# A selective-scan audio layer with routed experts: in the last group, the router of the group before, its scatters, the weight loads and a partial projection change their places

## The reference, cut to what matters

```python
h = tok(x)                                   # 64 x 128 x 256
h = h + attn(layernorm(h))                   # input projection, causal convolution of 4 taps, SiLU, then
                                             #   state = exp(delta*A)*state + delta*B*x ; y = sum(state*C)
                                             #   over 16 states and 512 channels, + D*x, * silu(z), @ W_out
h = h + ffn(layernorm(h))                    # 8 experts, each row goes to its best two:
# logits = x @ w_gate ; gates = softmax(logits) ; top_k(gates, 2)
# y_e = (silu(x @ wg[e]) * (x @ wi[e])) @ wo[e] ; out += gate_e * y_e
```

## Time and profile before

| | |
|---|---|
| median of 3 runs | 2734.6 us (2734.56 to 2735.72) |
| profiled execution, its own time | 2733.95 us |
| its span | 2732.2 us |
| busy share: TensorE, VectorE, ScalarE, GpSimd | 93%, 73%, 52%, 71% |
| first tile load of the expert stage | 1927.00 us |
| last group's last product ends | 1882.65 us |

### The profile page before, as it was taken

One profiled execution on the slowest core, in us unless ns is written; L12 is line 12 of the kernel. 1 busy time (PEld: TensorE's weight loads), 2 busy tenths in 40 slices (PEclk: granted clock), 3 DMA queues, 4 the chain that ended last, 5 costly groups with the idle time before them and its releaser, 6 DMA issues. The chain is left out here.

```text
span 2732.2 us, 29788 instructions
## 1 busy us (share of the span) xinstructions
PE 2539.4 (93%) x7976; PEld 1282.9 (47%) x7977; DVE 1984.1 (73%) x2171; ACT 1430.7 (52%) x2700; POOL 1945.9 (71%) x960
## 2 busy tenths in 40 slices
PE   4899999999999999999999999976799999999999
PEld 2234444444444444444444444433466666666665
DVE  1699999999999999999999999996222222222222
ACT  1666676766767667676676776752122222222222
POOL 1698999999999999999999999995222222222222
PEclk9999999999999999999999999988899999999999
DMA  1321413314133142241422414315222222222222
GB/s 42 140 113 42 153 60 126 136 34 158 64 117 144 30 157 90 89 148 35 154 110 62 151 39 147 128 39 208 66 46 44 43 45 41 46 45 42 46 44 31
DMA packets 125317, 236.03 MB, mean 86 GB/s; under 512 B 46289, under 2 KB 93426, under 8 KB 108834
## 3 DMA queue, kind: packets, MB, share of 16 engines
q1 hardware_dynamic: 98198, 200.42, 21.3%
q0 software_dynamic: 25984, 34.36, 7.3%
q10 hardware_dynamic: 1036, 0.09, 0.0%
HBM read 182.09 MB, written 53.65 MB: 86 GB/s over the span
## 5 line engine op out<-in xcount | busy, mean ns | idle before, releaser
L555 POOL TENSOR_TENSOR arena<-u,arena 128x2048 f32<-128x2048 f32 x255 | 1155.6, 4532 | 38.6 <-DVE psum L1069 34.5
L1069 DVE TENSOR_TENSOR_SCAN psum<-psum,arena 128x1024 f32<-128x1024 f32 x416 | 950.7, 2285 | 20.4 <-POOL arena L555 12.4
L1509 PE MATMUL psum<-hc,ident 128*128 128x512 f32 x1664 | 810.2, 610 | 106.0 <-DVE hc L1103 106.0
L831 ACT ACTIVATE psum<-delta,a_neg 128x508 f32<-128x508 f32 x1024 | 654.3, 670 | 0.0
L659 POOL DMA_INDIRECT out_dram<-hres,tok_id x135 | 210.1, 1556 | 595.0 <-ACT hres L996 541.1
L1509 PEld LDWEIGHTS psum<-hc,ident 128*128 128x128 f32 x1664 | 299.7, 191 | 508.7 <-issue 267.7
L1103 DVE TENSOR_TENSOR hc<-psum,arena 128x1024 f32<-128x1024 f32 x416 | 507.4, 1220 | 9.1
L1666 PE MATMUL psum<-arena,xnt 128*128 x1080 | 512.4, 597 | 0.0
L1370 DVE COPY z<-psum 128x512 f32<-128x512 f32 x135 | 93.4, 692 | 454.8 <-PE psum L1675 454.8
L825 ACT ACTIVATE psum<-zeros 128x8 f32<-128x8 f32 x512 | 90.3, 176 | 499.3 <-DVE hc L1103 451.2
L996 ACT ACTIVATE hres<-psum,tok_w 128x256 f32<-128x256 f32 x135 | 64.1, 474 | 451.1 <-PE psum L1685 444.4
(11 more groups left out here) (191 smaller groups left out, 2608.1 us busy)
## 6 DMA issues: line engine op xcount, KB each, us to landing
arena<-ssm_rows SPq DMA_DIRECT2D x128, 1024.0 KB, 5.5
delta<-expert_rows SPq DMA_DIRECT2D x135, 129.0 KB, 2.1
h_saved_rows<-hnew SPq DMA_DIRECT2D x16, 512.0 KB, 6.7
hres<-h_saved_rows SPq DMA_DIRECT2D x16, 512.0 KB, 3.5
out_dram<-h SPq DMA_DIRECT2D x16, 512.0 KB, 2.9
draw<-ssm_rows SPq DMA_DIRECT2D x16, 256.0 KB, 3.3
arena<-in_L_ffn_wg_dram SPq DMA_DIRECT2D x8, 512.0 KB, 10.1
arena<-in_L_ffn_wi_dram SPq DMA_DIRECT2D x8, 512.0 KB, 10.5
```

Of the source, the lines that this page charges most:

```text
L555: pool.tensor_tensor(dBx[k % 2], rep, b_rep[:, q * QN:(q + 1) * QN, :], ALU.mult).then_inc(dbx_ready, 1)
L831: last = nc.scalar.activation(o, d, ACT.Exp, scale=a_neg[:, c, n:n + 1])
L1069: nc.vector.tensor_tensor_scan(out_, h, src, 0.0, ALU.mult, ALU.add).then_inc(scan_done, 1)
L1509: last = nc.tensor.matmul(yacc[c % 2], ident[:, :], state[:, i, :], start=False, stop=(nth_sum[k] == LAST_SUM[c] and i == 1))
```

## The change

In the last group alone (`last`), the parts of group 14's router come four half units sooner on ScalarE, VectorE and TensorE (`sooner = 4`), with `norm2`'s second part at half unit 15 and not 16; count and slots, which stood at half unit 31 and in the tail, now stand inside the step at half units 27 to 29. The second partial projection moves from half unit 31, ahead of that unit's sum, to the tail, behind it. GpSimd's `tail` sends all eight scatters of group 14 ahead of the root of the last group. SyncE's first wait for the weight loads now also wants the first four scatters of group 14 to have landed.

```diff
--- before.py
+++ after.py
@@ -441,7 +441,7 @@
 
             def tail(g):
                 load_hres(g, G)
-                free_for(B_AT, (skip_done, NCH * G), (u_ready, NCH * G))
+                free_for(B_AT, (skip_done, NCH * G), (u_ready, NCH * G), (scattered, 16 * (2 * GB * (g - 1) + GB)))
                 free_for(C_AT, (dbx_ready, UN * G))
                 free_for(C_AT + 2 * QN * GT, (hc_ready, NOWN * G - 4), (hc_pool, NPL * G))
                 free_for(X_AT + SCN, (hc_ready, NOWN * G), (scan_done, HU * G))
@@ -639,10 +639,10 @@
                 first_row(g - 1)
                 scatter(g - 1, 0, 0)
                 scatter(g - 1, 0, 2)
-                rsqrt(g, 1, stat2, pow2)
                 second_row(g - 1)
                 scatter(g - 1, 1, 0)
                 scatter(g - 1, 1, 2)
+                rsqrt(g, 1, stat2, pow2)
                 scatter_last(g)
 
             pool.wait_ge(s_const, 9)
@@ -895,6 +895,7 @@
                 softplus_first()
 
             def step(g, par, first, second, more, last):
+                sooner = 4 if last else 0
                 for k in range(HU):
                     if k + 1 < HU:
                         exps(g, k + 1)
@@ -926,13 +927,13 @@
                             softplus_relu(g, 2)
                         if k == 7:
                             softplus_relu(g, 3)
-                        if k in (14, 16):
-                            norm2(g - 1, (k - 14) // 2)
-                        if k in (20, 22):
-                            evac_xn2t(g - 1, (k - 20) // 2)
-                        if k == 25:
+                        if k in ((14, 15) if last else (14, 16)):
+                            norm2(g - 1, int(k > 14))
+                        if k + sooner in (20, 22):
+                            evac_xn2t(g - 1, (k + sooner - 20) // 2)
+                        if k + sooner == 25:
                             router_exp(g - 1)
-                        if k == 30:
+                        if k + sooner == 30:
                             second_gate(g - 1)
                     if not last:
                         if k == 19:
@@ -1236,19 +1238,23 @@
                             residual(g - 1, 0)
                         if k == 10:
                             residual(g - 1, 1)
-                        if k == 24:
+                        if k + sooner == 24:
                             router_max(g - 1)
-                        if k == 26:
+                        if k + sooner == 26:
                             first_keys(g - 1)
-                        if k == 27:
+                        if k + sooner == 27:
                             one_hot(g - 1, 3, 0, dv)
-                        if k == 28:
+                        if k + sooner == 28:
                             second_max(g - 1)
                             exp_inverse(g - 1)
-                        if k == 29:
+                        if k + sooner == 29:
                             second_keys(g - 1)
-                        if k == 30:
+                        if k + sooner == 30:
                             one_hot(g - 1, 11, 1, mask_ready)
+                        if k + sooner == HU:
+                            positions(g - 1)
+                        if k + sooner == HU + 1:
+                            slots(g - 1)
                     if k == 30 and more:
                         aggregate(g + 2, 0, stat1)
                     times_c(g, k)
@@ -1257,17 +1263,22 @@
                             stats2(g - 1)
                         if k == 11:
                             aggregate(g - 1, 1, stat2)
-                        if k == 24:
+                        if k + sooner == 24:
                             router_sub(g - 1)
-                        if k == 26:
+                        if k + sooner == 26:
                             largest_key(g - 1, 2)
-                        if k == 27:
+                        if k + sooner == 27:
                             without_first(g - 1)
                             exp_sum(g - 1)
-                        if k == 28:
+                        if k + sooner == 28:
                             second_equal(g - 1)
-                        if k == 29:
+                        if k + sooner == 29:
                             largest_key(g - 1, 10)
+                        if k + sooner == HU:
+                            new_counts(g - 1)
+                            chosen_positions(g - 1)
+                        if k + sooner == HU + 1:
+                            slots_out(g - 1)
                     if not second:
                         if k == 0:
                             new_counts(g - 2)
@@ -1278,11 +1289,6 @@
                         stats1(g + 2)
 
             def tail(g):
-                positions(g - 1)
-                new_counts(g - 1)
-                chosen_positions(g - 1)
-                slots(g - 1)
-                slots_out(g - 1)
                 gate_y(g, NCH - 1)
                 residual(g, 0, bank_a)
                 residual(g, 1, yacc[0])
@@ -1616,19 +1623,19 @@
                         if k in (29, 30):
                             project_z(g + 1, k - 29, 2 * min(g + 3, G))
                     if not first:
-                        if k in (19, 21):
-                            turn_row(g - 1, (k - 19) // 2)
-                        if k == 23:
+                        if k + sooner in (19, 21):
+                            turn_row(g - 1, (k + sooner - 19) // 2)
+                        if k + sooner == 23:
                             router(g - 1)
-                        if k == 31:
+                        if k + sooner == 31:
                             count(g - 1)
                     if more:
                         if k in (22, 23):
                             turn_x(g + 2, k - 22)
                         if k in (24, 25):
                             embed(g + 2, k - 24)
-                    if last and k in (30, 31):
-                        project_out_last(g, k - 30, (0, 1, 2))
+                    if last and k == 30:
+                        project_out_last(g, 0, (0, 1, 2))
                     if k % HC == 0:
                         skip(g, par, k // HC)
                     if k not in ON_POOL:
@@ -1637,6 +1644,7 @@
                         add_state(g, DONE_WITH[k])
 
             def tail(g):
+                project_out_last(g, 1, (0, 1, 2))
                 for m in range(2):
                     project_out_last(g, m, (NCH - 1,))
                 pe.wait_ge(slot_ready, g)
```

## The result

The changed kernel takes 2739.28 us (median of 20 runs), the kernel before 2733.03 us beside it (20 runs): 6.25 us more, ratio 1.0023 with a 95% interval of 1.0017 to 1.0029. A part of the hit is luck. My range was set around the 2734.6 us of three runs of the kernel before, which is 1.6 above the median of its 20; taken as a difference it reached from -3.1 to +5.4 us, and the change cost 6.25.

A forecast was written before the change was run, and what follows sets the result against it. The last landing ahead of the first tile load was taken as the bound: scatters 1921.4, transfers 1928.1, the later counting, +1.9 us against 1926.2. That gave 2735.85 us for the profiled execution, median 2736.5, range 2731.5 to 2740.

The forecast's parts named there:

- What bounds: Ahead of the first expert tile: the whole effect is the shift of 1926.2, when all scatters, pads and weights have landed.
- Router sooner: Last group's step: VectorE pays 0.3 us, TensorE nothing; the earlier group's slots end at 1876.0 instead of 1884.23, 8.2 us sooner.
- Second projection behind the sums: TensorE's tail: last sum at 1883.0, projection hides the gate; residuals and statistics 0.9 us sooner, ready at 1891.9.
- Scatters ahead of the last root: GpSimd's tail: first four scatters landed at 1883.2, root at 1891.9, 4.8 us sooner; this chain alone ends at 1921.4.
- rival B: GpSimd's stall at a burst's second scatter returns; in the last burst +3 to +5 us, both bursts +7; chance 0.15.
- Weights held: SyncE's queue: 15.75 MB at 370 GB/s from 1883.4, plus 2.1 us, nothing idling, pads landing last at 1928.1.
- The sum: Ahead of the first tile load: the later of scatter chain 1921.4 and transfers 1928.1 counts, +1.9 us against 1926.2.
- Rival A: Transfers aren't the bound; the scatter chain sets the end at 1921.4 or a little after, 2729.8 us; chance 0.17.
- the sign of the forecast: Slower: +1.9 us at 370 GB/s; by the skill's 436 GB/s the change would gain 4.7 us.
- Rival C: Root does not move: 6.35 us landing waits, clock or code's place eat the gain; end 2736 to 2738; chance 0.06.

## Why the prediction was right, and where it was short

**What bounds.** Right. The first tile load is the one moment that counts, and with the hold its last wait goes from the scatters to the pads behind the weights. The hold alone on the kernel before moved the whole stream and left its length (47.1 and 46.95 us).

**Router sooner.** Right in every term: VectorE's extra 0.3 us, the slots' time, no price on TensorE. Alone it is worth 4.7 us. (The forecast's first load "instead of 1874.67" compares with the second expert's; the first expert's had left at 1857.20. The sum of the bytes had all 24 and isn't touched by this.)

**Second projection behind the sums.** The 0.9 us were there, but they aren't this edit's alone. Each edit gives them without the other: with their executions' own offsets taken out, the statistics are 0.8 us sooner with the router alone and 1.1 with the projection alone, and 0.9 with both. In the kernel's time the projection's share is nothing: without the router's move the root isn't waiting for the statistics, and with it they are as early anyway (2728.84 and 2729.03 us).

**Scatters ahead of the last root.** Here a step failed. "The first four then start at 1876.7, 1.28 us apart" took the 7.11 us gap for something that only weights in flight cause. The row of the kernel before showed a gap of no known cause, and I set it to zero where its cover was lighter, instead of taking it into the bounds. It came back as 3.33 us, 3.0 more than the ordinary 0.30, and since the hold waits for these scatters, every load and pad moved by it. The trace of the kernel before had a hint: the second scatter there started 1.8 us after the first one's landing, which by the 2.5 us that I took for a landing without weights gives a gap of about 3.2. The load's start was at 1887.0 and not 1883.4: 3.6 us, the other 0.6 being this execution's own offset. I had rival B at the right kind of place, the second scatter of a burst, but in the later bursts; it was in the first, where it is most expensive.

**Weights held.** The mechanism is right, one term was 1.5 us short. From the first load to the last landing it took 46.2 us (1886.96 to 1933.13) against my 44.7. The bytes were right (343 GB/s over the 46 us from 1887 to 1933 make 15.8 MB), and the rate of the full engines was higher than I took, 381 and not 370 GB/s. But I had the pads issued "before the backlog is through, so nothing idles". They were issued in 10.31 us, to 1930.56, not by 1921. The store of h2 landed at 1929.0 (1917.18 + 11.8); behind it the engines had only pads, one of 132 KB every 1.1 us, and moved 283 and then 150 GB/s. The last pad left alone and took its own 2.9 us.

**The sum.** 0.6 + 3.0 + 1.5 us make, but for rounding, the 5.0 us between my 1928.1 and the measured 1933.13. The first tile's matmuls gave 0.7 back. The profiled execution is thus 4.3 us above its forecast of 2735.85, and the median only 2.8 above 2736.5, because I had put the median 0.65 above the profiled execution; over 20 runs the medians lie 0.9 below it in the kernel before and 0.8 below it in the changed one.

**Rival A** is out by the chain of the changed kernel, which ends in a pad, and by the hold-only run. With it goes the time that the Trainium skill's rate gives.

By the Trainium skill ("DMA: Bandwidth & Descriptors", Anatomy of one DMA), 436 GB/s, the stream would have been over at an estimated 1921.5, level with the scatters, and the sign of the forecast would have turned. Rows of 36 us with full engines show 381 and 378 GB/s, so the page's fit for one transfer doesn't carry over to this mix.

**Rival C**, that landings among the weights take the root's gain back, held only without the hold: there the root started 7.6 us behind its statistics, and its place behind both bursts cost 7.2 us.

**The parts together.** Router alone -4.7; projection alone -0.1; order of the root alone +9.7; hold alone +15.6; all together +6.3. They don't add up, for two reasons. The router's move starts the scatters 8 us sooner, and with them whatever waits for them: the hold costs 15.6 us on the kernel before and about 10 on the kernel with router and projection (2729.03 to 2739.44). And the root's order and the hold lengthen two chains of which only the later counts: the order costs 7.2 us without the hold and nothing with it, the hold costs about 10 us without the order and some 3 with it. The hold does repair what the root's order breaks: with both, the root is on time. But neither is needed, for with slots at 1876 the first burst fits ahead of the statistics anyway. The change without its second half runs at 2728.8 to 2729.0 us.

## What to carry to other kernels

Ahead of a wait added to a queue, sum the bytes and the issues of everything behind it, not of the transfer that it is meant for: here 15.75 MB at 380 GB/s turned a chain 4 us shorter into an end 6 us later. When several edits go together, time each alone: one that only makes sense because of another can cost more than the first one won, and an order that is worth 7 us in one kernel is worth nothing where another wait ends last. A gap in a row without a known cause belongs in the bounds at every place that keeps its instruction, lighter load or not.

## What the runs showed of the hardware

- GpSimd's second indirect transfer of the first burst of four in a row starts 4.4 to 4.6 us after the first with idle engines and 7.9 to 8.6 us with full ones. Where the first one's landing is in the profile (five kernels), that is 1.8 to 1.9 us behind it. The later ones in a burst follow after 1.3 to 1.5 us, in full engines too; only the third of the last eight comes 2.1 to 2.2 us after the second. Pairs inside the groups don't show the gap. 24 instructions or 1 or 4 transfers more didn't move it.
- Full transfer engines moved 378 and 381 GB/s over 36 us in two kernels, with loads, a store and scatters in two queues. Giving the pads a third queue shortened the stream by 1.2 us only, and the weight loads issued beside them took 2.9 to 3.6 us each to issue instead of 1.5 to 1.8.
- A transfer whose address comes from a register was issued every 1.04 us by SyncE with idle engines (8.36 us for eight), and every 1.3 to 1.4 us (10.31 and 11.01 us) behind its own full queue. ScalarE, with nothing else in its queue, took 8.57 us for the eight among full engines.
